# Scattered expert rows: GpSimd's wait for the stores of the group before, where it waited for those of two groups back

## What is computed

```python
def _L1_ffn_ref(x, Wr, br, W1, b1, W2, b2):      # 64 experts, two per token
    logits = xf @ Wr + br
    topk_logits, topk_idx = jax.lax.top_k(logits, TOP_K)
    gates = jax.nn.softmax(topk_logits, axis=1)
    combine = zeros((T, E)).at[arange(T)[:, None], topk_idx].add(gates)
    for e in range(E):
        h = relu(xf @ W1[e] + b1[e])
        y = h @ W2[e] + b2[e]
        out = out + combine[:, e:e + 1] * y
```

## Time and profile before

| | |
|---|---|
| median of 3 runs | 2484.33 us (2482.07 to 2492.51) |
| profiled execution, its own time | 2486.96 us |
| its span, first to last instruction | 2485.1 us |
| POOL busy in the span | 1062.9 us (43%) |
| PE / DVE / ACT busy in the span | 1843.3 / 1667.6 / 1113.8 us |
| expert stage, POOL's stores (L1501) | x224, 215.3 us busy, 217.9 us idle before them |

### The profile page before, as it was taken

How to read it: one execution, slowest core, us unless ns; L and a number is a source line. 1 busy time by engine, 2 the same in 40 slices (tenths; PEclk the granted TensorE clock), 3 DMA queues, 4 the chain that set the end, 5 groups by cost and what they waited for, 6 DMA issues and landing times.

```text
span 2485.1 us, 55409 instructions
## 1 busy us (share of the span) xinstructions
PE 1843.3 (74%) x17723; PEld 1432.8 (58%) x17723; DVE 1667.6 (67%) x5137; ACT 1113.8 (45%) x3614; POOL 1062.9 (43%) x846
## 2 busy tenths in 40 slices
PE   5888887999999999999997477774333336666662
PEld 2367775777777777777775255553212225555551
DVE  0067773588888888888886699996888843333334
ACT  2477762344444444444443398873212123444340
POOL 0056650134344444434433222212777755445553
PEclk9889996899999999999996588876555555555555
DMA  9910000000000000000000000005000031111114
GB/s 289 279 45 0 0 1 1 2 2 2 1 0 0 0 0 0 0 0 0 0 0 1 0 1 1 1 0 190 22 22 21 22 93 36 35 35 37 36 29 163
DMA packets 79641, 84.93 MB, mean 34 GB/s; under 512 B 53792, under 2 KB 68256, under 8 KB 78240
## 3 DMA queue, kind: packets, MB, share of 16 engines
q1 hardware_dynamic: 66064, 66.50, 9.5%
q0 software_dynamic: 13312, 13.85, 1.7%
q10 hardware_dynamic: 144, 3.15, 0.3%
HBM read 55.78 MB, written 27.69 MB: 34 GB/s over the span
## 4 chain that ended last, share of the span: by engine, by line
PE 34%; DVE 22%; issue 18%; POOL 14%; DMA 4%; another core or an unknown queue 4%; ACT 3%; DVEq 1%; POOLq 0%; SPq 0%; ACTq 0%
POOL routed_rows L1488 8%; PE PS L698 5%; PE PS L992 5%; DMA arena<-in_x_dram 4%; PE PS L665 3%; PE PS L732 3%; POOL rstd L1389 3%; PE PS L713 3%; PE PS L1002 2%; DVE XR L1642 2%; DVE XR L1842 2%; DVE XR L1638 1%; PE PS L747 1%; PE PS L772 1%
## 5 line engine op out<-in xcount | busy, mean ns | idle before, releaser
L1112 ACT ACTIVATE arena<-PS 128x384 f32<-128x384 f32 (+2 forms) x376 | 162.7, 451 | 342.6 <-remote 147.6
L1501 POOL DMA_INDIRECT expert_rows<-arena x224 | 215.3, 961 | 217.9 <-DVE arena L2044 155.8
L1638 DVE TENSOR_REDUCE XR<-PS 128x2 f32<-128x192 f32 (+2 forms) x768 | 173.8, 280 | 104.7 <-PE PS L698 104.7
L1488 POOL DMA_INDIRECT routed_rows<-XR,SLu x192 | 208.9, 1088 | 81.1 <-issue 77.8
L2024 DVE TENSOR_TENSOR arena<-PS,XR 128x512 f32<-128x512 f32 x56 | 38.7, 692 | 295.9 <-PE PS L992 199.5
L698 PE MATMUL PS<-arena 32*128 32x96 f32 (+2 forms) x3072 | 234.3, 285 | 0.0
L992 PE MATMUL PS<-arena,XR 64*128 64x64 f32 x896 | 148.8, 410 | 89.8 <-issue 89.0
L698 PEld LDWEIGHTS PS<-arena 32*128 32x128 f32 x3072 | 198.5, 192 | 20.6
L1359 ACT ACTIVATE XR<-arena 128x257 f32 x448 | 153.3, 407 | 111.3 <-issue 90.7
L1148 ACT ACTIVATE XR<-PS 128x256 f32<-128x256 f32 x512 | 167.2, 381 | 67.3 <-PE PS L713 67.1
L1434 POOL TENSOR_TENSOR arena<-arena,mhalf 96x16 f32<-96x16 f32 x32 | 93.3, 2914 | 241.6 <-DVE arena L1684 241.6
(11 more groups left out here) (309 smaller groups left out, 4693.8 us busy)
## 6 DMA issues: line engine op xcount, KB each, us to landing
arena<-in_x_dram SPq DMA_DIRECT2D x32, 784.0 KB, 10.5
arena<-in_t_experts_dram SPq DMA_DIRECT2D x8, 1028.0 KB, 12.3
routed_rows<-zt SPq DMA_DIRECT2D x14, 528.0 KB, 5.8
arena<-routed_rows SPq DMA_DIRECT2D x56, 132.0 KB
expert_rows<-arena POOLq DMA_INDIRECT x224
WP<-in_t_pack_dram SPq DMA_DIRECT2D x1, 3428.5 KB, 20.4
mixed_rows<-Hb SPq DMA_DIRECT2D x4, 768.0 KB
routed_rows<-XR,SLu POOLq DMA_INDIRECT x192
```

Of the source, the lines that this page charges most:

```text
L1112: return act.activation(dst, src, ACT.Identity, **kw)
L1488: pool.indirect_dma_start(XD, bass.IndirectOffsetOnAxis(SLu[:, u, k, b:b + 1], 0), XG[:, u, b, k, :], None).then_inc(scat[u], 16)
L1501: pool.indirect_dma_start(YD, bass.IndirectOffsetOnAxis(yi[:, u % 4, k:k + 1], 0), yb[:, u % 4, k, :], None).then_inc(e_st[u % 2], 16)
L1638: dve.tensor_reduce(negmax[:, p, j, :], PS[:, S_:S_ + 2, S_AT[j]:S_AT[j] + QB * (j + 1)], AX_X, ALU.max, negate=True).then_inc(b_max, 1)
```

## The change

Before the four stores of group g, `e_back` waited for `e_y` of g and for the stores of g−2 (the semaphore of its own parity). Now it waits as well for the semaphore of the other parity, which stands at the stores of g−1:

```diff
                 pool.wait_ge(e_y, g + 1)
                 wait(pool, e_st[u % 2], (g - u % 2) * 32)
                 pool.sem_inc(go, 1)
+                wait(pool, e_st[1 - u % 2], (g + u % 2) * 32)
+                pool.sem_inc(go, 1)
                 for k in range(KB):
                     pool.indirect_dma_start(YD, bass.IndirectOffsetOnAxis(yi[:, u % 4, k:k + 1], 0),
                                             yb[:, u % 4, k, :], None).then_inc(e_st[u % 2], 16)
```

## The result

The changed kernel takes 2453.39 us (median of 4 runs, 2450.92 to 2461.87) beside 2487.38 for the kernel before (4 runs, 2482.07 to 2492.51). The ratio is 0.9899, with a 95% interval of 0.9873 to 0.9926. So the change gains 1.0 to 1.3% there; the forecast was 47 us, or 1.9%.

What follows compares the result with a forecast made beforehand. POOL works in bursts, then starves for `e_y` while its stores slow the others. 55 groups × 6.62 + 3.84 = 368.0 us against 416.5, −48.5; plus 1.5 for stalls, −47: 2437 us, own range 2424 to 2451, ended at 2474.

Steps and rivals of the forecast that it cites:

- the slow stretch: Expert stage: from 5.0 to 11.5 us after a burst's first store, everybody but POOL nearly stands, 6.6 of 15.1 us.
- the second: POOL's wait between groups: 3.84 us of stores, 2.00 landing, 0.78 restart, 6.62 us a group; alone a 43 us loss.
- the stalls that were put down: POOL in the expert stage: 1.5 us added for one or two stalls like the 2.22 us one at 2256.86.
- The third step: Expert stage: four stores take a shared path 5.7 us; the pause frees some 0.9 us a group, so POOL sets pace.
- The added instructions cost nothing: POOL's added increment and wait instruction: under 5 us in all, counted as nothing because earlier stores are still in flight.
- Rival B: Expert stage: the pause helps but engines miss 6.62 us; 7.0 to 7.4 us a group, 2456 to 2478 us; chance 0.13.
- the prediction's point against the page of the Trainium skill: Store landings: by the page's fixed DMA cost of about 2.0 us alone, waiting for each is a loss, +43 us.
- `e_y` isn't waited for any more: POOL's wait for DVE's line 2044 ends: `e_y` is there at 8.2 us, needed at 13.2; gaps of about 1.8 us.
- Rival A: Expert stage: the slow stretch does not shorten, belonging to something once a cycle like code loading; +43 us, 2527; chance 0.13.
- Rival C: POOL's new wait: nothing happens, since it would already be satisfied when POOL comes to it; chance 0.05.

Runs made afterwards that it cites:

- h2_after: The changed kernel again, in a second, longer comparison on a first-kind chip: 2450.42 us beside 2483.41 for the kernel before, ratio 0.9869.
- h1_before: The kernel before, unchanged, run again for its trace on a first-kind chip: 2484.59 us, ratio 1.0005.
- e1: The kernel before with no new wait but one 128x1056 memset on POOL behind each group's four stores: 2487.77 us, ratio 1.0005.
- f2: The kernel before with two memsets (128x1056 and 128x384) behind each group's stores, no landing wait, first-kind chip: 2431.59 us, ratio 0.9790.
- h3: The kernel before with two memsets (128x1056 and 128x128) behind each group's stores, no landing wait, first-kind chip: 2481.86 us, ratio 0.9994.
- f3: The kernel before with two memsets (128x1056 and 128x640) behind each group's stores, no landing wait, first-kind chip: 2428.95 us, ratio 0.9781.
- i1_before: The kernel before, unchanged, profiled on a chip of the second kind: 2349.09 us, ratio 0.9999.

## Why the prediction was right and where it was wrong

On the first kind of chip the direction was right, and so was what the mechanism needed there: time without stores shortens the slow stretch. The size was off: 34 us by the medians (25 by the ratio), not 47. The step that failed is the second, 6.62 us a group. Measured were 6.80, and nearly four times the stalls that were put down, so the stage came out 32.4 us shorter and not 48.5. The third step had no condition on the length of the pause, which the experiments found; and on the second kind of chip the third step is false and the direction was wrong.

1. *The added instructions cost nothing.* The two of them are under 0.05 us each in the chain of the changed kernel, ahead of a restart that waits anyway. That fits the profile; it wasn't tried alone.

2. *A group takes POOL 6.62 us.* **This is the term that was mis-sized.** The chain of the changed kernel near the stage's end:

```profile
2425.59 2.12 DMA expert_rows<-arena
2427.71 0.02 issue
2427.74 0.02 POOLq L1501
2427.75 0.74 issue
2428.49 0.96 POOL expert_rows L1503
```

The restart is 0.74 + 0.04 us, as put. The landing is 2.12 here where one row, 2.00, had been taken for all; in the groups just before it is up to 2.16. The median from start to start over the stage is 6.80 us: 0.18 × 55 = 9.9 us. Four groups took longer (7.63, 7.36, 8.72 and 9.35 us), 5.9 us over the median together, where 1.5 had been put down for stalls. The last two hold a stall of POOL before a group's second store (1.28 and 2.12 us, ended by "issue"), like the one of the earlier trace rows. That makes 6.80 × 55 + 3.85 + 5.9 = 383.8 us, measured 384.1; forecast 368.0. Rival B had this part as a restart delayed by a slow step; most of it was the landing. That a landing can be waited for at 2 us each and yet pay was the prediction's point against the page of the Trainium skill, "DMA: Bandwidth & Descriptors", section "Anatomy of one DMA — SWDGE (gpsimd) path". Its fixed cost of about 2.0 us holds, at 2.1 to 2.2 us here; what the prediction drew from it alone, a loss, holds on the second kind of chip (+4.1%) and not on the first.

The rest of the distance between the profiled runs, which differ by 25.1 us and not by the stage's 32.4, lies ahead of the stage: its first store came at 2048.2, and at 2040.8 before. In h2_after and h1_before it came at 2034.5 and 2034.3, so those 7 us are no part of the change. There the stage went from 415.8 to 385.3 us and the median from 2484.59 to 2450.42.

3. *Each store takes a common path for 1.43 us, and a pause frees it.* Partly shown for the first kind. The release came 5.74 to 5.77 us after the first of four stores in the rows of e1, f2 and h3, and in the changed kernel 46 of 56 relus start 5.70 to 5.94 us after it. Time without stores gives the gain with no wait for a landing at all (f2, f3). That it is one path, taken by each store in turn, stays inferred. The landing of a burst's last store can't be the release: after eight stores it is due at 8.90 + 2.1 = 11.0 us and the release came at 11.5, after eleven at 14.8 and the release came at 15.8. Two things were wrong. The prediction took any free time as enough ("the path is free for some 0.9 us in every group"), and by it a pause of 0.2 or 0.3 us would have gained as well; e1 and h3 gained nothing. The 1.0 us of the changed kernel was over the step, and that was luck: the length of a landing set it. And the others are held up earlier than 5.0 us into a burst: in the changed kernel PE's product ends 3.22 us in (2204.80), and DVE starts on it 2.6 us later. It costs nothing there, since POOL sets the pace. On the second kind the whole step is false, which the trace of before, from one chip, could not tell.

4. *`e_y` isn't waited for any more.* Right: 17.0 us in 4 waits, PE and DVE as had been named, and a median gap of 1.98 us instead of 1.8.

Rival A fell: PE doesn't crawl in the changed kernel's rows. Its page of the Trainium skill, "Runtime: NRT & Kernel Launch", section "Instruction fetch mechanics", says that engines can stall on their streamed code. Code loads as often on the second kind, with no slow stretch; its two rows from 2040 to 2322 us of i1_before answer to the earlier trace rows:

```profile
q14 instruction: 31, 0.25, 0.3%
q8 instruction: 5, 0.08, 0.1%
```

Rival C fell by the 55 waits. The rival that was missing is that the stores hold nobody up, POOL is the bound, and each of 55 waits adds 1.76 us: +97 us, as on the second kind.

Two small slips of the prediction change nothing: the slow stretch from 2060.94 to 2067.46 is 6.5 us and not 6.6, and A has a chance of 0.13 in one place and of 0.14 in the other.

**What stays open.** What the path is, and why the chips differ, no run here shows. A rival that no run tests is the recording itself. On the first kind three quarters of the landings of the kernel before have no record, and every time on record comes with the span and the granted clock of a trace. The recording may take part in the slow stretch, or only suffer from it; the way to tell is to time both kernels without it, on both kinds of chips, and until then the gain of 1.0 to 1.3% is, as far as the record tells, one of recorded runs. That the 1.43 us belong to a store and not to its 128 rows isn't settled either: stores of fewer rows were not tried. The step lies between 0.30 and 0.53 us by two kernels; what sets it was read from their timelines and not tested by changing what PE has under way.

**The best of them.** On the first kind f2_two384 and f3_two640, a pause of issue without the landing, beat the changed kernel by about 20 us: 2431.59 and 2428.95 beside 2450 to 2453, each against its own chip's before. On the second kind none beats the kernel before (2349).

## What to carry to other kernels

When several engines idle at once with nothing named that they wait for, and it begins and ends with another engine's stream of DMAs, measure the price of one such DMA from bursts of two lengths. Then try gaps of several lengths: here 0.16 and 0.30 us of free time gave nothing and 0.53 us all of it, so one short pause that fails proves little. Put the gap inside the burst, not at its edge. Before such a pause goes into a kernel, time it on more than one chip: it is worth only as much as the disturbance that it avoids, and where there was none it cost its full length. And look whether the traces are as complete on one chip as on the other; if they aren't, ask first whether the disturbance is there without them.

## What was not expected of the hardware

- Two kinds of chips, for one kernel on one core: 2481 to 2487 us and 2349 to 2350 us, five per cent, nearly all of it in one stage (416.5 and 283.6 us).
- On one kind the other engines come free 5.7 to 5.9 us after the first of four scattered stores of 128 rows, 11.5 us after the first of eight and 15.8 after the first of eleven, which is 1.43 us a store that is issued every 1.26 us; on the other kind PE doesn't stand still beside them. The changed kernel takes nearly the same time on both (2450 to 2453, and 2447).
- A step between 0.30 and 0.53 us of free time, from no gain (0.9994 [0.9979, 1.0010]) to the full one (0.9790 [0.9746, 0.9834]).
- The same kernel leaves 846 of 3584 records of its stores' landings on one kind and 3473 on the other, while a store's packets start 1.5 us after it on both.
